# Graph attention kernel, second layer: absent pairs through TensorE, the search for a block's top in four parts, the negation on GpSimd, three loads issued during the projection

## The chip, the cores and the metric

The kernel runs on one core of one Trainium2 chip. The metric is the device time of one execution in microseconds (us), of which the median over several runs is taken.

## The reference

6250 nodes with 128 channels, 200000 edges sorted by target. Two graph attention layers, each followed by a layer norm of input plus layer. The change lies in the second layer (`_L1_gnn_ref`), with 4 heads of 32 channels:

```python
H = jnp.matmul(x, W).reshape(n, HEADS, OUT_DIM).transpose(1, 0, 2)
H_s = jnp.einsum('hnd,hd->hn', H, A_left[..., 0])
H_t = jnp.einsum('hnd,hd->hn', H, A_right[..., 0])
s = H_s[:, src] + H_t[:, tgt]
s = jnp.where(s >= 0, s, ALPHA * s)
s = jnp.exp(s - jnp.max(s))
denom = jnp.zeros((HEADS, n), dtype=s.dtype).at[:, src].add(s)
alpha = s / (denom[:, src] + EPS)
agg = jnp.zeros((HEADS, n, OUT_DIM), dtype=H.dtype).at[:, src].add(alpha[..., None] * H[:, tgt])
agg = agg + jnp.matmul(x, residual_projection).reshape(n, HEADS, OUT_DIM).transpose(1, 0, 2)
```

and an elu, the sum with the input and the norm behind it. The kernel subtracts a top per block of source nodes instead of one global maximum, and corrects the small constant in the denominator for it at the end.

## The kernel before, in words

The 6250 nodes lie in 49 blocks of 128. An early stage sorts the edges into pairs of blocks (source block b, target block n); an edge of a pair gets one of 128 lanes, and a lane without an edge is an absent pair, marked by -1 in the table `SL`. Stages follow one another with a barrier between them: loading, binning, scores of the first layer, sums of the first layer (`layer0_sums`), `norm_and_project` (L1036), which turns the normed nodes and multiplies them by the weights of the second layer, `layer1` (L1157), and `elu_and_norm`.

`layer1` works in 343 steps: for each of the 49 source blocks b, 7 steps of 7 target blocks each (`GX = 7`, `PER = 7`). Five engines run their own hand-written order and meet through semaphores:

- **SP** (L1191) loads, for step u, the lanes' node numbers of 7 source-target pairs, spread to all 128 partitions (448 KB), into a ring of three (`LOADS`). Load u waits until the one-hot of step u-3 is made.
- **VectorE** (L1265): in iteration t it makes the one-hot of step t+10 (`make`, L1209), in one iteration in seven searches the top of a block (`find_top`, L1212), weighs the gathered rows by the softmax weights (`weigh`, L1244), compares lanes (`find_lanes`, L780), in one in seven negates the block's top (`negate`, L1233), and takes the low half of three messages (`take_low`, L1252). `find_top` for block b stands in iteration 7b-2, ahead of `weigh`: it marks absent lanes by -1e30 (L1217), reduces the three parts of the scores out of two PSUM banks (L1219, twice), takes max(0.2 s, s) (L1225), adds the marks (L1227) and takes the maximum over the free axis (L1228).
- **GpSimd** (L1280): for each block the all-reduce of the top over the partitions (L1289), then for block b-1 two additions of low sums (L1283, L1284), which wait for ScalarE's copies, then the subtraction of 1 from X (L1292).
- **TensorE** (L1343): in iteration t the scores of step t+9 (`add_scores`, 14 matmuls of 12 columns, L1306 and L1307), the gather of step t+1 (21 matmuls of 128 columns, L1316), the sums of step t (`add_up`, 4 matmuls in fp32, L1330, of which the last needs ScalarE's last message, and 3 matmuls of halves, L1335). The first scores of a block wait until `find_top` of the block before has read the banks.
- **ScalarE** (L1399): in iteration t the high halves (L1379), the message of the seventh target block (`weigh_last`, 4 instructions, L1385), in one iteration in seven the exponent (L1361, it waits for the negated top), the copy of weights (L1370), the widening of the lane one-hots to fp32 (L1374); once per block the staging of the block's lanes (L1354) and the taking of the sums (L1393 to L1395).

`weigh` of a block's first step waits for the exponent. TensorE's `add_up` waits for `weigh`, and TensorE, VectorE and ScalarE are at most two steps apart through double buffers for gathered rows, messages and lane one-hots. The one-hots have a ring of 11.

A first matmul with `start=True` opens a bank's sums; later ones with `start=False` add.

## Time and profile before

| | |
|---|---|
| median of 3 runs | 3372.64 us (3370.05 to 3385.1) |
| the profiled execution | 3371.61 us, its span 3369.8 us |
| mean granted TensorE clock | 0.968 |
| busy: TensorE, weight loads, VectorE, ScalarE, GpSimd | 91%, 83%, 92%, 81%, 5% |
| `layer1` | 2274 to 3315 us |
| `norm_and_project` | 2232 to 2274 us |

The profile shows one execution. Busy time is that of instructions; PE is TensorE's matmuls, DVE VectorE, ACT ScalarE, POOL GpSimd. A granted clock of 1.00 is 2.4 GHz, 0.50 is 1.2 GHz. "Issue" is time in which an engine waited for nothing that the profile shows. Instructions on one engine overlap at their ends, so a start-to-start distance is a little shorter than a duration.

### The profile page before, as it was taken

The numbers are of one execution on the slowest core, as the hardware profiler recorded it, in microseconds if no ns is written. First come the engines' busy times: TensorE is split into PE (matmuls) and PEld (weight loads), VectorE is DVE, ScalarE is ACT, GpSimd is POOL, SyncE is SP. The second block draws the span as 40 slices with busy tenths as digits, with TensorE's granted clock in tenths as the row PEclk, the third lists the DMA queues.
The fourth block names the chain that finished last, engine by engine and source line by source line (L and its number), as shares of the span: only waits on it lengthen the run. The fifth ranks groups of instructions, "written<-read, shape, count | busy, mean of one in ns | idle before, by whom it ended". The sixth has DMA issues, their size and how long they took to land. (4 is left out here: it accounts for less than half of the span.)

```text
span 3369.8 us, 100973 instructions
## 1 busy us (share of the span) xinstructions
PE 3073.6 (91%) x39974; PEld 2791.6 (83%) x39974; DVE 3095.1 (92%) x5054; ACT 2725.8 (81%) x6802; POOL 159.1 (5%) x252
## 2 busy tenths in 40 slices
PE   4777689999999999699999999987999999999995
PEld 3666577777777777599999999977999999999994
DVE  7999879998999999899999999978999999999997
ACT  4989777777877777699999999975777777777777
POOL 0000000000000000000000000000111111111110
PEclk9999899999999999799999999998999999999998
DMA  2000022222222222244333333305444445444441
GB/s 63 12 15 12 9 96 90 84 90 85 90 84 85 90 84 72 55 96 96 97 97 97 96 97 97 96 30 182 159 156 156 158 156 158 157 156 158 156 144 40
DMA packets 173164, 333.01 MB, mean 99 GB/s; under 512 B 54849, under 2 KB 108693, under 8 KB 172690
## 3 DMA queue, kind: packets, MB, share of 16 engines
q1 hardware_dynamic: 172690, 326.50, 31.6%
q8 instruction: 321, 5.26, 0.6%
q14 instruction: 153, 1.25, 0.1%
HBM read 320.77 MB, written 5.66 MB: 97 GB/s over the span
## 5 line engine op out<-in xcount | busy, mean ns | idle before, releaser
L942 PE MATMUL l_gathered<-xp,l_src_onehot 128*128 128x128 bf16 x7203 | 466.9, 221 | 11.2 <-DVE l_src_onehot L855 11.2
L647 PE MATMUL sc_z<-sc_onehot,pq 128*128 128x256 f32 (+1 forms) x2450 | 426.5, 296 | 54.5 <-DVE sc_leaky L568 44.9
L1316 PE MATMUL l_gathered<-hp,l_onehot 128*128 128x128 bf16 x7203 | 459.0, 219 | 0.0
L736 ACT ACTIVATE sc_leaky<-sc_z 128x1024 f32<-128x1024 f32 (+3 forms) x325 | 310.1, 954 | 153.0 <-PE sc_z L651 96.3
L942 PEld LDWEIGHTS l_gathered<-xp,l_src_onehot 128*128 128x128 bf16 x7203 | 407.8, 99 | 26.2 <-DVE l_src_onehot L855 11.6
L780 DVE TENSOR_TENSOR l_lane<-iota_b,l_lane_pairs 128x896 bf16<-128x896 bf16 x686 | 421.7, 615 | 0.0
L1330 PE MATMUL l_acc<-e,l_lane_wide 128*128 128x132 f32 x2744 | 399.3, 286 | 16.5 <-ACT e L1385 16.3
L568 DVE SCALAR_TENSOR_TENSOR sc_leaky<-sc_z,sc_leaky 128x1024 f32<-128x1024 f32 (+3 forms) x325 | 369.9, 1138 | 45.6 <-ACT sc_leaky L736 42.2
L1316 PEld LDWEIGHTS l_gathered<-hp,l_onehot 128*128 128x128 bf16 x7203 | 406.7, 98 | 0.4
L651 PE MATMUL sc_z<-sc_onehot,pq 128*128 128x256 f32 (+1 forms) x2450 | 401.0, 286 | 0.0
L647 PEld LDWEIGHTS sc_z<-sc_onehot,pq 128*128 128x128 f32 x2450 | 340.7, 194 | 69.3 <-issue 68.2
L1330 PEld LDWEIGHTS l_acc<-e,l_lane_wide 128*128 128x128 f32 x2744 | 338.4, 190 | 32.9 <-ACT e L1385 25.9
L1379 ACT CAST l_message_halves<-e 128x396 fp32r<-128x396 f32 x343 | 179.2, 522 | 213.2 <-DVE e L1244 211.6
L651 PEld LDWEIGHTS sc_z<-sc_onehot,pq 128*128 128x128 f32 x2450 | 345.7, 196 | 0.0
L1244 DVE TENSOR_TENSOR e<-l_gathered,l_weight 128x768 f32<-128x768 f32 x343 | 326.8, 953 | 10.7 <-PE l_gathered L1316 3.9
L1374 ACT CAST l_lane_wide<-l_lane 128x896 fp32r<-128x896 bf16 x343 | 329.1, 959 | 0.0
L988 ACT CAST l_lane_wide<-l_lane 128x896 fp32r<-128x896 bf16 x343 | 322.2, 939 | 4.0 <-DVE l_lane L780 4.0
L559 DVE TENSOR_SCALAR sc_onehot<-placed,part 128x1536 fp32r<-128x1536 uint8 (+3 forms) x325 | 310.8, 957 | 3.8 <-DMA placed<-edge_rows 3.7
L953 PE MATMUL l_acc<-l_messages,l_lane_wide 128*128 128x128 f32 x2058 | 305.9, 285 | 5.7 <-ACT l_messages L997 5.7
L997 ACT ACTIVATE l_messages<-l_gathered,e 128x128 f32<-128x128 f32 x1029 | 301.5, 363 | 0.0
L869 DVE TENSOR_TENSOR l_message_halves<-l_messages,l_message_halves 128x512 fp32r<-128x512 f32 x343 | 237.5, 692 | 53.1 <-ACT l_message_halves L1003 48.3
L1385 ACT ACTIVATE e<-l_gathered,l_weight 128x32 f32<-128x32 f32 x1372 | 280.6, 286 | 0.0
(233 smaller groups left out, 6064.3 us busy)
## 6 DMA issues: line engine op xcount, KB each, us to landing
l_got<-edge_rows_wide SPq DMA_DIRECT2D x343, 448.0 KB, 3.7
l_got<-edge_rows_src SPq DMA_DIRECT2D x343, 224.0 KB, 3.2
placed<-edge_rows SPq DMA_DIRECT2D x144, 512.0 KB, 3.7
out_dram<-X SPq DMA_DIRECT2D x12, 256.0 KB
edge_rows<-bin_bytes SPq DMA_DIRECT2D x98, 6.1 KB
edge_rows_wide<-bin_rows SPq DMA_DIRECT2D x98, 12.2 KB
placed<-edge_rows SPq DMA_DIRECT2D x24, 64.0 KB, 2.8
placed<-edge_rows SPq DMA_DIRECT2D x6, 256.0 KB, 3.6
```

The source lines that it names most:

```text
L559: nc.vector.tensor_scalar(hot[:, r % HOTS, 0:early, :, 0:nw, :], bytes_of(r)[:, 0:early, :, 0:nw, :], k.part1[:, 0:1], None, ALU.is_equal) ...
L568: nc.vector.scalar_tensor_tensor(out=y, in0=z, scalar=ALPHA, in1=y, op0=ALU.mult, op1=ALU.add).then_inc(s["leaky"], 1)
L647: nc.tensor.matmul(z[:, b, 0:nw, :], PQ[:, b0 + b, q, 0:C], hot[:, r % HOTS, b, 0, 0:nw, :], start=(b == u and q == 0), stop=False)
L651: ins = nc.tensor.matmul(z[:, u:u + v, n, :], PQ[:, 2 * pair + n, q, C:2 * C], hot[:, r % HOTS, u:u + v, 1, n, :], start=False, stop=(n == ...
L736: nc.scalar.activation(y, z, ACT.Relu, scale=1.0 - ALPHA).then_inc(s["positive"], 1)
L780: return nc.vector.tensor_tensor(out.rearrange("p i (u v) -> p i u v", v=2), k.iota_b[:].rearrange("p (u v) -> p u v", v=2).unsqueeze(1).t ...
L942: ins = nc.tensor.matmul(gps[:, t % 2, i * P:(i + 1) * P], hot[:, t % RING, i, :], parts[:, g * GX + i, q, :], start=(q == 0), stop=(q == 2))
L988: nc.scalar.copy(lane_wide[:, t % 2], lane[:, t % 2]).then_inc(s["lane_wide"], 1)
L1244: nc.vector.tensor_tensor(msg[:, t % 2, 0:w, 0:C].rearrange("p i (e d) -> p i e d", e=HEADS), gps[:, t % 2, 0:w * P].rearrange("p (i e d) ...
L1316: ins = nc.tensor.matmul(gps[:, t % 2, i * P:(i + 1) * P], dst_hot[:, t % RING, i, :], hp[:, g * GX + i, q, 0:C], start=(q == 0), stop=(q ...
L1330: nc.tensor.matmul(acc[:, b % 2, 0:CW], lane_wide[:, t % 2, i, :].bitcast(F32), msg[:, t % 2, i, :], start=(g == 0 and i == SPLIT), stop=F ...
L1374: nc.scalar.copy(lane_wide[:, t % 2], lane[:, t % 2]).then_inc(s["lane_wide"], 1)
```

## The change

Absent lanes are no longer marked on VectorE. ScalarE makes a bf16 tile `absent` (Relu of the negated `SL`: 1 where a lane is absent, 0 elsewhere), once per block and two blocks ahead. TensorE opens each bank of scores with one matmul of that tile (28 or 21 target blocks by 4 heads) against -1e30 times the identity, and the score matmuls add to it. So the leaky step takes the mark with it.

The search is taken apart: the reduction of the first bank in iteration 7b-4, its leaky half in 7b-3, the reduction and leaky half of the second bank and the maximum in 7b-2, all behind `weigh`; the maximum is the last of its iteration. The semaphore `read` becomes two, one per bank.

The negation goes from VectorE to GpSimd, behind the all-reduce. The first three loads of `layer1` are issued by SP at the start of `norm_and_project`; their tile and semaphores are allocated outside `layer1`.

```diff
--- before.py
+++ after.py
@@ -1033,7 +1034,14 @@
 
-def norm_and_project(nc, k, X, mean_var, hp, R):
+def load_rows(sp, k, got, wide_rows, u):
+    b, g = divmod(u, NBK // GX)
+    sp.dma_start(got[:, u % LOADS_1].rearrange("p a x -> p (a x)"),
+         wide_rows[g, 2 * b:2 * b + 2].rearrange("a i l -> (a i l)").partition_broadcast(P)
+         ).then_inc(k.rows_loaded[u % LOADS_1], 16)
+
+
+def norm_and_project(nc, k, X, mean_var, hp, R, got, wide_rows):
@@ -1060,6 +1068,11 @@
 with nc.Block() as block:
+    @block.sync
+    def _(sp):
+        for u in range(LOADS_1):
+            load_rows(sp, k, got, wide_rows, u)
+
@@ -1168,13 +1181,13 @@
 s = {n: ctx.semaphore("l1_" + n) for n in (
-    "chain", "const", "hot", "scored", "read", "top", "all", "negated", "exp", "staged", "lane", "lane_wide", "gathered",
+    "chain", "const", "hot", "scored", "absent", "first_read", "last_read", "first_lifted", "last_lifted", "top", "all", "negated", "exp", "staged", "lane", "lane_wide", "gathered",
     "messages", "last_message", "weights", "high", "low", "added", "taken", "summed")}
-loaded = [ctx.semaphore(f"l1_loaded{h}") for h in range(LOADS)]
-got = sb("got", [P, LOADS, 2, GX * P], BF16)
+loaded = k.rows_loaded
...
 src_hot, dst_hot = hot[:, 0:2], hot[:, 2:]
-win, absent = sb("lane_pairs", [P, 2, NB, 2], BF16), sb("absent", [P, NB])
+win = sb("lane_pairs", [P, 2, NB, 2], BF16)
+absent, never = sb("absent", [P, 2, NB], BF16), sb("never", [P, P], BF16)
@@ -1187,13 +1200,9 @@
     def _(sp):
-        for u in range(R):
-            b, g = divmod(u, PER)
-            if u >= LOADS:
-                sp.wait_ge(s["hot"], u - LOADS + 1)
-            sp.dma_start(got[:, u % LOADS].rearrange("p a x -> p (a x)"),
-                         wide_rows[g, 2 * b:2 * b + 2].rearrange("a i l -> (a i l)").partition_broadcast(P)
-                         ).then_inc(loaded[u % LOADS], 16)
+        for u in range(LOADS, R):
+            sp.wait_ge(s["hot"], u - LOADS + 1)
+            load_rows(sp, k, got, wide_rows, u)
@@ -1209,29 +1218,39 @@
 
-        def find_top(b):
-            dve.wait_ge(s["staged"], b + 1)
-            dve.wait_ge(s["scored"], (b + 1) * PER)
+        def take_scores(b, bank, i, j):
+            nc.vector.tensor_reduce(
+                parts[:, i:j, :], sps[:, bank, 0:(j - i) * HP].rearrange("p (i q e) -> p i e q", q=3, e=HEADS),
+                AX.X, ALU.add).then_inc(s["last_read" if bank else "first_read"], 1)
+
+        def lift(b, bank, i, j):
+            dve.wait_ge(s["last_read" if bank else "first_read"], b + 1)
...
                 dve.wait_ge(s["exp"], b - 1)
-            nc.vector.tensor_scalar(absent[:], win[:, b % 2, :, 0], 0.0, NEVER, ALU.is_lt, ALU.mult)
-            for bank, i, j in ((0, 0, FIRST), (1, FIRST, NB)):
-                ins = nc.vector.tensor_reduce(
-                    parts[:, i:j, :], sps[:, bank, 0:(j - i) * HP].rearrange("p (i q e) -> p i e q", q=3, e=HEADS),
-                    AX.X, ALU.add)
-            ins.then_inc(s["read"], 1)
-            dve.wait_ge(s["read"], b + 1)
-            flat, sc = parts[:].rearrange("p i e -> p (i e)"), score[:, b % 2]
-            ch.link(nc.vector.scalar_tensor_tensor(out=sc.rearrange("p i e -> p (i e)"), in0=flat, scalar=ALPHA, in1=flat,
-                                                   op0=ALU.mult, op1=ALU.max))
-            ch.link(nc.vector.tensor_tensor(sc, sc, absent[:].unsqueeze(2).to_broadcast([P, NB, HEADS]), ALU.add))
-            nc.vector.tensor_reduce(top[:, b % 2:b % 2 + 1], sc.rearrange("p i e -> p (i e)"), AX.X, ALU.max
+            flat = parts[:, i:j, :].rearrange("p i e -> p (i e)")
+            nc.vector.scalar_tensor_tensor(out=score[:, b % 2, i:j, :].rearrange("p i e -> p (i e)"), in0=flat, scalar=ALPHA,
+                                           in1=flat, op0=ALU.mult, op1=ALU.max
+                                           ).then_inc(s["last_lifted" if bank else "first_lifted"], 1)
+
+        def take_first(b):
+            dve.wait_ge(s["scored"], b * PER + FIRST // GX)
+            if b >= 1:
+                dve.wait_ge(s["first_lifted"], b)
+            take_scores(b, 0, 0, FIRST)
+
+        def take_last(b):
+            dve.wait_ge(s["scored"], (b + 1) * PER)
+            if b >= 1:
+                dve.wait_ge(s["last_lifted"], b)
+            take_scores(b, 1, FIRST, NB)
+
+        def find_top(b):
+            dve.wait_ge(s["first_lifted"], b + 1)
+            dve.wait_ge(s["last_lifted"], b + 1)
+            if b >= 2:
+                dve.wait_ge(s["all"], b - 1)
+            nc.vector.tensor_reduce(top[:, b % 2:b % 2 + 1], score[:, b % 2].rearrange("p i e -> p (i e)"), AX.X, ALU.max
                                     ).then_inc(s["top"], 1)
-
-        def negate(b):
-            dve.wait_ge(s["all"], b + 1)
-            nc.vector.tensor_scalar(neg[:, b % 2:b % 2 + 1], k.m_all[:, b:b + 1], -1.0, None, ALU.mult
-                                    ).then_inc(s["negated"], 1)
@@ -1259,22 +1278,29 @@
 
+        nc.vector.tensor_scalar(never[:], k.ident_b[:], NEVER, None, ALU.mult).then_inc(s["const"], 1)
...
                 make(t + AHEAD + 1)
+            if t >= 0:
+                weigh(t)
+            if (t + 4) % PER == 0 and 0 <= (t + 4) // PER < NB:
+                take_first((t + 4) // PER)
+            if (t + 2) % PER == 0 and 0 <= (t + 2) // PER < NB:
+                take_last((t + 2) // PER)
+            if 0 <= t + 1 < R:
+                find_lanes(t + 1)
+            if (t + 3) % PER == 0 and 0 <= (t + 3) // PER < NB:
+                lift((t + 3) // PER, 0, 0, FIRST)
+            if (t + 2) % PER == 0 and 0 <= (t + 2) // PER < NB:
+                lift((t + 2) // PER, 1, FIRST, NB)
+            if t >= 0:
+                take_low(t)
...
                 find_top((t + 2) // PER)
-            if t >= 0:
-                weigh(t)
-            if 0 <= t + 1 < R:
-                find_lanes(t + 1)
-            if (t + 1) % PER == 0 and 0 <= (t + 1) // PER < NB:
-                negate((t + 1) // PER)
-            if t >= 0:
-                take_low(t)
@@ -1283,10 +1309,15 @@
 
-        pool.wait_ge(s["const"], 1)
+        pool.wait_ge(s["const"], 2)
...
             nc.gpsimd.partition_all_reduce(k.m_all[:, b:b + 1], top[:, b % 2:b % 2 + 1], P, RMAX).then_inc(s["all"], 1)
+            pool.wait_ge(s["all"], b + 1)
+            if b >= 2:
+                pool.wait_ge(s["exp"], b - 1)
+            nc.gpsimd.tensor_scalar(neg[:, b % 2:b % 2 + 1], k.m_all[:, b:b + 1], -1.0, None, ALU.mult
+                                    ).then_inc(s["negated"], 1)
@@ -1294,17 +1325,31 @@
     def _(pe):
+        def exclude(b, bank, i, j):
+            nc.tensor.matmul(sps[:, bank, 0:(j - i) * HP].rearrange("p (i c) -> p i c", c=HP)[:, :, 0:HEADS], never[:],
+                             absent[:, b % 2, i:j].unsqueeze(2).to_broadcast([P, j - i, HEADS]), start=True, stop=False,
+                             skip_group_check=True)
+
...
             b, g = divmod(u, PER)
+            if g == 0:
+                pe.wait_ge(s["absent"], b + 1)
+                if b >= 1:
+                    pe.wait_ge(s["first_read"], b)
+                exclude(b, 0, 0, FIRST)
+            if g == FIRST // GX:
+                if b >= 1:
+                    pe.wait_ge(s["last_read"], b)
+                exclude(b, 1, FIRST, NB)
             pe.wait_ge(s["hot"], u + 1)
-            if g == 0 and b >= 1:
-                pe.wait_ge(s["read"], b)
...
                 o = sps[:, bank, at * HP:(at + 1) * HP]
-                nc.tensor.matmul(o, dst_hot[:, u % RING, i, :], hp[:, n, :, C + HEADS:C + 2 * HEADS], start=True, stop=False)
-                ins = nc.tensor.matmul(o, src_hot[:, u % 2, i, :], hp[:, b, :, C:C + HEADS], start=False, stop=True)
+                nc.tensor.matmul(o, dst_hot[:, u % RING, i, :], hp[:, n, :, C + HEADS:C + 2 * HEADS], start=False, stop=False,
+                                 skip_group_check=True)
+                ins = nc.tensor.matmul(o, src_hot[:, u % 2, i, :], hp[:, b, :, C:C + HEADS], start=False,
+                                       stop=(n in (FIRST - 1, NB - 1)), skip_group_check=True)
@@ -1337,6 +1382,7 @@
 
+        pe.wait_ge(s["const"], 1)
@@ -1350,8 +1396,12 @@
                 act.wait_ge(s["lane"], (b - 1) * PER)
-                act.wait_ge(s["top"], b - 1)
             nc.scalar.copy(win[:, b % 2], k.SL[:, 0, 0:NB, b].unsqueeze(2).to_broadcast([P, NB, 2])).then_inc(s["staged"], 1)
+
+        def find_absent(b):
+            if b >= 2:
+                act.wait_ge(s["scored"], (b - 1) * PER)
+            nc.scalar.activation(absent[:, b % 2], k.SL[:, 0, 0:NB, b], ACT.Relu, scale=-1.0).then_inc(s["absent"], 1)
@@ -1394,6 +1444,8 @@
 
+        find_absent(0)
+        find_absent(1)
@@ -1406,6 +1458,8 @@
                 widen(t + 1)
+            if t >= 0 and (t - 2) % PER == 0 and (t - 2) // PER + 2 < NB:
+                find_absent((t - 2) // PER + 2)
```

## Rows read from the trace of the kernel before

**Rows 1.** Busy time by stretch: start:end, length, busy (instructions) per engine, PEclk, DMA share, GB/s
```profile
2400.00:2600.00 200.00, 196.99 (x3109) 190.45 (x3106) 194.37 (x336) 158.89 (x526) 25.36 (x39) 1.00 0.49 158
```

**Rows 2.** Waits, 2330 to 3270 us: engine line <- releaser: us, times, longest
```profile
PE l_acc L1330 <- ACT e L1385: 15.1, 45, 0.3
```

**Rows 3.** PE timeline, one block: start us, us, engine line (idle before)
```profile
2788.77 1.33 PE L1316 MATMUL l_gathered<-hp,l_onehot 128*128 128x128 bf16 x21
...
2791.64 1.33 PE L1316 MATMUL l_gathered<-hp,l_onehot 128*128 128x128 bf16 x21
...
2795.28 1.33 PE L1316 MATMUL l_gathered<-hp,l_onehot 128*128 128x128 bf16 x21
```

**Rows 4.** DVE timeline, the search of one block and an ordinary step
```profile
2789.92 0.19 DVE L1217 TENSOR_SCALAR l_absent<-l_lane_pairs 128x49 f32<-128x49 bf16 x1
2790.01 0.83 DVE L1219 TENSOR_REDUCE l_score_parts<-l_scores 128x112 f32<-128x336 f32 x2
2790.87 0.36 DVE L1225 SCALAR_TENSOR_TENSOR l_score<-l_score_parts 128x196 f32<-128x196 f32 x1
...
2791.66 0.36 DVE L1228 TENSOR_REDUCE l_top<-l_score 128x1 f32<-128x196 f32 x1
2791.94 0.95 DVE L1244 TENSOR_TENSOR e<-l_gathered,l_weight 128x768 f32<-128x768 f32 x1
...
2797.22 0.96 DVE L1244 TENSOR_TENSOR e<-l_gathered,l_weight 128x768 f32<-128x768 f32 x1
...
2798.77 0.57 DVE L1252 TENSOR_TENSOR l_message_halves<-e,l_message_halves 128x396 fp32r<-128x396 f32 x1
...
2799.85 0.95 DVE L1244 TENSOR_TENSOR e<-l_gathered,l_weight 128x768 f32<-128x768 f32 x1
```

**Rows 5.** ACT timeline, the exponent and the last messages of a step
```profile
2796.66 0.47 ACT L1361 ACTIVATE l_weight<-l_score,l_negated 128x196 f32<-128x196 f32 x1
...
2798.64 0.82 ACT L1385 ACTIVATE e<-l_gathered,l_weight 128x32 f32<-128x32 f32 x4
```

**Rows 6.** POOL timeline, blocks 0 and 1
```profile
2295.91 0.60 POOL L1289 PARTITION_ALL_REDUCE block_top<-l_top  x1 [65.56 <-DVE l_top L1228]
2305.07 0.92 POOL L1292 TENSOR_SCALAR X<-X 128x128 f32<-128x128 f32 x1 [8.55 <-issue]
2313.62 0.38 POOL L1289 PARTITION_ALL_REDUCE block_top<-l_top  x1 [7.63 <-DVE l_top L1228]
2324.97 0.76 POOL L1283 TENSOR_TENSOR S<-S,l_low_sums 128x128 f32<-128x128 f32 x1 [10.97 <-ACT den L1395]
```

**Rows 7.** Source lines of GpSimd: xcount, duration ns min/median/max, first and last start
```profile
L1283 POOLq MODIFY_POOL_CONFIG  x96: 82/83/83, 2314.0 to 3291.6; - x96
...
L1284 POOL TENSOR_TENSOR den<-den,l_low_sums x49: 203/522/527, 2325.7 to 3314.6; 128x4 f32<-128x4 f32 x49
...
L1289 POOLq MODIFY_POOL_CONFIG  x98: 5/7/11, 2274.8 to 3284.8; - x98
...
L1292 POOLq MODIFY_POOL_CONFIG  x2: 83/83/83, 2296.5 to 2296.5; - x2
```

**Rows 8.** DVE timeline, start of the layer: first and ninth one-hot, first weighing
```profile
2278.84 0.69 DVE L1209 TENSOR_SCALAR l_onehot<-l_got,part 128x1792 bf16<-128x1792 bf16 x1 [3.76 <-DMA l_got<-edge_rows_wide]
...
2292.98 0.69 DVE L1209 TENSOR_SCALAR l_onehot<-l_got,part 128x1792 bf16<-128x1792 bf16 x1 [1.41 <-DMA l_got<-edge_rows_wide]
...
2297.83 0.96 DVE L1244 TENSOR_TENSOR e<-l_gathered,l_weight 128x768 f32<-128x768 f32 x1 [0.36 <-PE l_gathered L1316]
```

**Rows 9.** PE around the gap before the projection: start:end, length, busy, PEclk, DMA share, GB/s
```profile
2222.00:2229.00 7.00, 6.70 (x76) 1.00 0.01 2
...
2235.00:2238.20 3.20, 3.00 (x13) 0.50 0.00 0
```

**Rows 10.** PE timeline, the same gap
```profile
2235.20 1.67 PE L1105 MATMUL np_turned_ps<-ident,X 128*128 128x128 f32 x6 [5.84 <-DVE X L1069]
```

**Rows 11.** ACT timeline, last stage
```profile
3339.03 1.28 ACT L2254 ACT_TABLE_LOAD   x1
```

More of the change, by code:

```diff
@@ L100 @@
 GX = 7
+LOADS_1 = 3
 R_BYTES = 4 * P
@@ L1154, in _, with layer1 @@
                     take_middle(g)
-def layer1(nc, k, hp, wide_rows, spare, X, S, den4):
+def layer1(nc, k, hp, got, wide_rows, spare, X, S, den4):
     NB, PER, AHEAD = NBK, NBK // GX, 9
     R = NB * PER
-    RING, LOADS = AHEAD + 2, 3
+    RING, LOADS = AHEAD + 2, LOADS_1
     CW, HP, FIRST = C + HEADS, 3 * HEADS, 28
@@ L2307, in gnn_program @@
         k.x_loaded = ctx.semaphore("x_loaded")
+        k.rows_loaded = [ctx.semaphore(f"rows_loaded{h}") for h in range(LOADS_1)]
         k.w1_all = sb("w1_all", [P, 2 * C + 2 * HEADS])
@@ L2344, in binned_layer1 @@
                 hp = scope.enter_context(nc.sbuf_tensor("hp", [P, k.NI, 3, C + 2 * HEADS], BF16))
-                norm_and_project(nc, k, X, mean_var, hp, R)
-                layer1(nc, k, hp, wide_rows, e0[:].rearrange("p a b -> p (a b)"), X, S, den4)
+                got = scope.enter_context(nc.sbuf_tensor("rows_got", [P, LOADS_1, 2, GX * P], BF16))
+                norm_and_project(nc, k, X, mean_var, hp, R, got, wide_rows)
+                layer1(nc, k, hp, got, wide_rows, e0[:].rearrange("p a b -> p (a b)"), X, S, den4)
         either(nc, "layer0", binned, 1, binned_layer0,
```

## The prediction

> **What bounds the kernel now.** I read the busy time by stage first, then the waits, then the timelines of one block. The change touches the second layer (2274 us to the end) and the first microseconds of the projection before it. In a stretch of 200 us inside that layer TensorE is busy 197.0 us and VectorE 194.4 us at a granted clock of 1.00, while GpSimd has 25 us of work [rows 1]. So TensorE and VectorE are both nearly full, and who waits for whom decides. The only repeated wait of TensorE is for ScalarE's last message, once per block [rows 2].
>
> The PE timeline gives the size. From one gather to the next takes 2.87 us (2788.77 to 2791.64); in the step with the search it takes 3.64 us (2791.64 to 2795.28) [rows 3]. A block is 7 steps: 6 x 2.86 + 3.64 = 20.80 us, of which 0.78 us is loss, 48 times.
>
> The DVE timeline says why [rows 4]. An ordinary VectorE step takes 2.63 us (2797.22 to 2799.85), less than TensorE's. But the search is one unbroken run ahead of the weighing: 2789.92 to 2791.94, 2.02 us. From the start of a weighing ScalarE needs 2.24 us until its last message is made (2797.22 to 2798.64 + 0.82) [rows 4, 5]. The search makes the weighing about 1.8 us late, TensorE loses 0.78 us, so some 1.0 us of lateness is free.
>
> **The search, part by part.** Removed from VectorE per block: the comparison L1217 (0.19), the addition L1227 (as long as the leaky step beside it), the negation, and the waits between dependent instructions. Kept: two reductions (0.83 together), the leaky step (0.36, now in two halves, between 0.18 and 0.36 each; I take 0.25 for the first and 0.2 for the second), the search for the top (0.36) [rows 4]. They now lie in three steps, and none stands before the weighing of its own step. The most added between two weighings is 0.36 + 0.2 + 0.36 = 0.9 us, in the third of these steps, after VectorE has gained 0.23 us on TensorE in each step without them. That stays under the free 1.0 us. Taken alone this removes all of the 0.78 us: 48 x 0.78 = 37 us.
>
> **Absent pairs on TensorE.** Two matmuls per block, with 112 and 84 columns. The gather does 21 matmuls of 128 columns in 1.33 us, its end included, 0.06 each [rows 3]; by columns the two cost 0.09 us. The floor is zero (hidden in a stall), the ceiling 0.78 us, the whole gain of the search part: two matmuls would then cost more than half a gather, which nothing suggests. I take 0.09, the nearest shape: 49 x 0.09 = 4.4 us if TensorE bounds. Their buffers are released two steps earlier (reads of scores) and three (the rectified row), so their waits cost nothing unless VectorE is more than two steps behind; then the scores and gathers queued behind them on TensorE would wait too.
>
> **The Relu on ScalarE**, 49 columns, is smaller than the exponent (196 columns, 0.47 us [rows 5]), once a block. ScalarE is idle for 41 of 200 us [rows 1], some 0.6 us per step, and the Relu stands in a step that has neither staging, exponent nor taking. I take nothing; if that cover went, it would be at most 0.47 x 49 = 23 us. Relu and Exp alternate in the last stage with no table load until L2254 asks for Sqrt [rows 11], so no table is reloaded. If it were, two loads of 1.28 us per block would come.
>
> **Loads issued early.** Today the first one-hot is made at 2278.84 and the ninth at 2292.98, each after its load [rows 8]. With three loads there already, the first is made at about 2275.1, and the fourth load is issued some 3.6 us sooner; the spacing after that is the loads' own. The ninth one-hot then comes at about 2289.4. SP issues nothing else during the projection and nothing in it waits for a DMA; the three transfers (448 KB each) have some 40 us to land, so they cost nothing. They also pass no other queue; if they were late, the first one-hot would wait as before. The first top is found at about 2290.9 in place of 2295.69 (the end of the ninth one-hot, 2293.67, and the 2.02 us of the search).
>
> **The negation on GpSimd.** This is the term that decides. Before, a block's top goes VectorE, GpSimd (all-reduce), VectorE (negation), ScalarE (exponent). The negation moves onto GpSimd, right behind the all-reduce. In the trace GpSimd runs two instructions MODIFY_POOL_CONFIG ahead of each all-reduce (98 at L1289) and two more right after it, booked on the next ordinary instruction (96 at L1283, 2 at L1292) [rows 7]. So it changes its code twice per block. What does the change back cost? Once the trace shows it: in block 0 nothing is waited for, the all-reduce ends at 2296.51, and L1292 starts at 2305.07 after 8.55 us of "issue" [rows 6]. From block 1 on, the next ordinary instruction waits 10.97 us for ScalarE anyway [rows 6], which hides 8.55 us. The new negation has no such cover: behind it stand ScalarE's exponent, then VectorE's weighing L1244 of the block's first step, then TensorE's sum.
>
> Is 8.55 us paid once or in each block? For each block: the four instructions recur in all 49, and ordinary code had been in use before (the first layer's additions on GpSimd, L928), so its return was not a first load. For once: only one exposed case. I take 8.55 each time.
>
> The Trainium skill, GPSIMD Engine Reference, section Instruction dispatch, says that the first call to a freshly loaded kernel additionally pays about 6 us (5.95 measured) with no visible instruction. The mechanism agrees with the trace, the size does not; by 5.95 the sum below, without its clock term, would be about 3506 us, an estimate.
>
> **The chain.** Let a block's first weighing start at 0. VectorE reaches the weighing of its sixth step (the one with the end of the search) after 5 x 2.63 = 13.15 us plus 0.3 (of the 0.7 us of first reduction and first leaky half, 0.4 us lies in the gap that the subtraction L1252, starting 1.55 us after its weighing, leaves while it waits for ScalarE) [rows 4]: 13.45. From there to the end of the top: 1.55 + 0.4 + 0.49 + 0.36 = 2.8, so 16.25. Then: 0.14 for the hand-over to GpSimd, 0.38 for the all-reduce [rows 6], 8.56 for the code, 0.3 for the negation (bounds 0.20 and 0.52, a 4-column addition on GpSimd [rows 7]), 0.47 for the exponent [rows 5], some 0.1 for hand-overs: 9.95. The next block's first weighing starts at 26.2 us, where TensorE alone would need 7 x 2.86 + 0.09 = 20.12.
>
> **The clock.** TensorE then idles some 5.8 us in each block. A gap of the same length stands in the trace: after 5.84 us without a matmul it resumed at 2235.20, and the granted clock was 0.50 (1.2 GHz) until 2238.2, 3.0 us more; before the gap it had been busy at 2.4 GHz [rows 9, 10]. Half of 3.0 us is 1.5 us of lost work; 0.6 us of it falls into the wait for the last message, 0.2 us into VectorE's own lateness; 0.7 us stays. Bounds: 0 (clock up again at once) and 2.2 us (low for twice as long). Period: 26.95 us.
>
> **The sum.** Start of the layer: top at 2290.9, + 0.2 + 0.60 + 8.56 + 0.3 + 0.47 + 0.1 gives the first weighing at 2301.15, where it was at 2297.83 [rows 8]: +3.3 us (the 4.7 us won by the loads go into the code change). Then 48 x (26.95 - 20.80) = +295 us. 3371.6 + 298 = 3670 us. The profiled execution stands 1 us below the median of the three runs, so no correction is due. With no clock loss it is 3371.6 + 3.3 + 48 x 5.4 = 3634; with the upper clock bound 3742. If the change of code took 7.3 us in later blocks (the all-reduce's own comes ready in at most the 7.63 us that GpSimd idles before it in block 1 [rows 6]), it is about 3610.
>
> **Rivals.**
> - *The code returns for free after the first time* (8%). For it: only one exposed case; against it: the recurring instructions [rows 7]. Then the start still costs 3.3 us, and each block runs at 20.12 us: 48 x 0.68 = 33 us gained, 3371.6 + 3.3 - 32.6 = 3342 us. Faster. The point that decides: the chain is 26.2 - 8.56 = 17.65 us and the code's time; it passes TensorE's 20.12 us from 2.5 us on, and each further microsecond costs 48.
> - *The return costs something between* (4%), 4 to 7 us, because later loads run faster than the one seen: 3410 to 3590 us; slower.
> - *The negation is cheap, but a new wait or the two matmuls eat the gain* (2%): TensorE waits for the rectified row or for the split reads; 0.7 us per block puts it at 3365 to 3380, no change.
>
> **How the numbers follow.** The forecast has 86%. Its own range covers 7.3 to 8.9 us of code change and 0 to 2.2 us of clock loss: 3560 to 3760, which holds it 19 times in 20, so 8 times in 10 in all. A measurement of this kernel tells 0.5% (17 us) from no change. Faster: 8% for the free return, and 2% for a cover that I overlooked. Same: 2%. Slower: 88%.
>
> **What would show it.** After the change: on GpSimd the negation preceded by some 8.5 us of "issue" in all 49 blocks; ScalarE's exponent waiting for GpSimd, 6 us each; VectorE's L1244 waiting for the exponent; TensorE idle 5 to 6 us per block with the granted clock at 0.50 in patches, a mean below 0.9 in a layer that shows 1.00 now; no more wait of 0.33 us in the search step; the first one-hot at 2275. The forecast is wrong if the "issue" appears only once: then the time is below the one of before. It is wrong in size if the clock stays at 1.00 or falls for longer.

## The result, and the profile after

| | before | after |
|---|---|---|
| median of 6 runs each, us | 3373.30 (3368.47 to 3390.03) | 3684.76 (3681.21 to 3687.29) |
| ratio, 95% interval | | 1.0924 [1.0904, 1.0944] |
| profiled run, us (span) | 3371.61 (3369.8) | 3681.21 (3679.4) |

The changed kernel is 311 us slower; 3670 had been forecast, between 3560 and 3760.

Busy time by stretch, kernel after (start:end, length, busy (instructions) of PE, PEld, DVE, ACT, POOL, then PEclk, DMA share, GB/s), the same stretch as [rows 1]:

```profile
2400.00:2600.00 200.00, 161.77 (x2312) 157.79 (x2313) 141.14 (x239) 122.60 (x405) 14.91 (x36) 0.86 0.35 117
```

Every engine has lost work in the same time, and the granted clock is 0.86 where it was 1.00. No engine is full, so the layer is now bound by a chain of waits. They are, from 2400 to 3400 us (us in total, times, longest):

```profile
POOL l_negated L1319 <- issue: 287.1, 37, 8.5
...
DVE e L1263 <- issue: 230.1, 37, 7.0
ACT l_weight L1411 <- POOL l_negated L1319: 227.6, 37, 6.9
...
PE l_acc L1375 <- ACT l_lane_wide L1424: 178.4, 37, 5.6
```

These are four views of one event. 37 blocks lie in that stretch, and each line stands 37 times. GpSimd stands idle before the negation without a wait that the trace shows, 287.1 / 37 = 7.76 us each; ScalarE's exponent waits 6.2 us for that negation; VectorE's first weighing waits 6.2 us (shown as "issue"; in block 0, below, the profile names the exponent); TensorE's sum waits 4.8 us. [Rows 2] had 45 waits of 0.33 us in its place.

The GpSimd timeline, kernel after, blocks 0 to 2 (start us, us, engine line operation, in brackets the idle time before it):

```profile
2285.93 0.38 POOL L1315 PARTITION_ALL_REDUCE block_top<-l_top  x1 [59.28 <-DVE l_top L1252]
2293.49 0.26 POOL L1319 TENSOR_SCALAR l_negated<-block_top 128x1 f32<-128x1 f32 x1 [7.17 <-issue]
...
2311.89 0.69 POOL L1315 PARTITION_ALL_REDUCE block_top<-l_top  x1 [17.61 <-DVE l_top L1252]
2320.66 0.26 POOL L1319 TENSOR_SCALAR l_negated<-block_top 128x1 f32<-128x1 f32 x1 [8.08 <-issue]
...
2339.11 0.70 POOL L1315 PARTITION_ALL_REDUCE block_top<-l_top  x1 [10.19 <-DVE l_top L1252]
2347.41 0.26 POOL L1319 TENSOR_SCALAR l_negated<-block_top 128x1 f32<-128x1 f32 x1 [7.60 <-issue]
```

This answers [rows 6]. There the idle time before the next ordinary instruction was called "issue" only in block 0; now it is in every block. The two instructions MODIFY_POOL_CONFIG that [rows 7] shows at L1283 have moved to the negation's line, 98 of them, two for each of the 49 blocks (source lines of GpSimd: count, duration ns min/median/max, first and last start):

```profile
L1319 POOLq MODIFY_POOL_CONFIG  x98: 82/83/83, 2286.3 to 3595.1; - x98
L1319 POOL TENSOR_SCALAR l_negated<-block_top x49: 260/260/261, 2293.5 to 3602.2; 128x1 f32<-128x1 f32 x49
```

One block boundary on VectorE, kernel after: the end of the search, the first weighing of the next block, the top after that, and the weighing behind it:

```profile
2611.39 0.35 DVE L1252 TENSOR_REDUCE l_top<-l_score 128x1 f32<-128x196 f32 x1
...
2621.76 0.96 DVE L1263 TENSOR_TENSOR e<-l_gathered,l_weight 128x768 f32<-128x768 f32 x1 [6.80 <-issue]
...
2639.01 0.35 DVE L1252 TENSOR_REDUCE l_top<-l_score 128x1 f32<-128x196 f32 x1
...
2648.58 0.96 DVE L1263 TENSOR_TENSOR e<-l_gathered,l_weight 128x768 f32<-128x768 f32 x1 [6.00 <-issue]
```

The chain closes here. From the end of one top (2611.74) to the weighing it releases is 10.0 us, from that weighing to the end of the next top (2639.36) 17.6 us, then 9.2 us again. On the mean of blocks 2 to 46 the two stretches are 9.45 and 17.85 us. The mean distance between the starts of the all-reduces of blocks 2 to 46, which I call the period, is 27.30 us, and was 20.81 us. 48 x 6.49 = 311 us, the whole difference.

### The profile page after: what moved, and what is told of

Read it like the earlier page. It is cut to its first block and busy times, and to the rows that moved or that the text cites. A ratio compares the mean times of both kernels' runs of the same rounds, so it can differ in the third digit from the quotient of the medians.

```text
span 3679.4 us, 101361 instructions
## 1 busy us (share of the span) xinstructions
PE 3169.8 (86%) x40072; PEld 2894.6 (79%) x40072; DVE 3055.4 (83%) x4957; ACT 2737.1 (74%) x6851; POOL 135.8 (4%) x301
## 5 line engine op out<-in xcount | busy, mean ns | idle before, releaser
L1375 PE MATMUL l_acc<-e,l_lane_wide 128*128 128x132 f32 x2744 | 433.1, 306 | 237.9 <-ACT l_lane_wide L1424 237.6
L1375 PEld LDWEIGHTS l_acc<-e,l_lane_wide 128*128 128x128 f32 x2744 | 378.2, 211 | 245.2 <-DVE e L1263 244.7
L1361 PE MATMUL l_gathered<-hp,l_onehot 128*128 128x128 bf16 x7203 | 502.2, 230 | 0.0
L1361 PEld LDWEIGHTS l_gathered<-hp,l_onehot 128*128 128x128 bf16 x7203 | 448.9, 104 | 0.5
```

The source lines that it names most:

```text
L1361: ins = nc.tensor.matmul(gps[:, t % 2, i * P:(i + 1) * P], dst_hot[:, t % RING, i, :], hp[:, g * GX + i, q, 0:C], start=(q == 0), stop=(q ...
L1375: nc.tensor.matmul(acc[:, b % 2, 0:CW], lane_wide[:, t % 2, i, :].bitcast(F32), msg[:, t % 2, i, :], start=(g == 0 and i == SPLIT), stop=F ...
```

## The experiments

Theory A: the change of GpSimd's code back to ordinary instructions, behind each all-reduce, costs 7 to 8.5 us and stands on the path once it has no cover; the half clock that follows adds to it. Rival B: something else in the change (the matmuls for absent pairs, the split search, the early loads) costs the time. Rival C: the cost is that of any second instruction on GpSimd, or of one more hand-over to it, and not of the change of code.

All ratios are to the kernel before, run beside them on the same chip (medians 3373.3, 3368.7, 3369.6 and 3369.1 us). The period is reckoned from the trace of one execution, as above. Medians of different groups can differ by a few us, as those of the kernel before do, so small differences between runs are read from the period and not from the medians alone.

| run | us, median | ratio [95%] | period, us |
|---|---|---|---|
| after | 3684.76 | 1.0924 [1.0904, 1.0944] | 27.30 |
| neg_dve | 3331.40 | 0.9889 [0.9870, 0.9907] | 20.11 |
| before_neg_pool | 3572.24 | 1.0582 [1.0552, 1.0612] | 24.91 |
| two_reduces | 3331.65 | 0.9888 [0.9871, 0.9904] | 20.10 |
| warm | 3612.69 | 1.0723 [1.0705, 1.0741] | 25.74 |
| late_loads | 3337.61 | 0.9897 [0.9877, 0.9917] | 20.11 |
| one_search | 3343.33 | 0.9926 [0.9901, 0.9951] | 20.37 |
| split_only | 3332.95 | 0.9886 [0.9865, 0.9906] | 20.07 |
| lead | 3477.23 | 1.0305 [1.0274, 1.0337] | 23.11 |
| neg_act | 3329.83 | 0.9884 [0.9868, 0.9901] | 20.11 |
| act_marks | 3324.71 | 0.9874 [0.9857, 0.9890] | 20.01 |

**neg_dve: the changed kernel with the negation back on VectorE.**

```
-  pool.wait_ge(s["all"], b + 1)              # GpSimd, behind the all-reduce
-  pool.wait_ge(s["exp"], b - 1)
-  nc.gpsimd.tensor_scalar(neg..., k.m_all..., -1.0, None, ALU.mult).then_inc(s["negated"], 1)
+  def negate(b):                             # VectorE, in the step before the block
+      dve.wait_ge(s["all"], b + 1)
+      nc.vector.tensor_scalar(neg..., k.m_all..., -1.0, None, ALU.mult).then_inc(s["negated"], 1)
```

> The changed kernel with only the negation put back on VectorE, between the lane comparison and the low halves of the step before the exponent. Theory (the change back to ordinary code on GpSimd, some 7.8 us, is on the path once per block): all of the loss goes and the rest of the change shows its gain: start of the layer about 5 us shorter, block period 20.12 us in place of 20.80, so 3335 us, 3325 to 3345; no idle gap of TensorE over 1 us in the layer, clock 1.00. Rival (matmuls of absent pairs, split reads or Relu cost something too): the time stays above 3345. Rival (GpSimd's part is only a share of the loss, the split search breaks something else): above 3400.

Measured: 3331.40 us. One instruction per block of 128 x 1 elements on another engine is worth 353 us, and without it the change is a gain of 37 us. Busy time by stretch, neg_dve:

```profile
2400.00:3200.00 800.00, 800.00 (x12898) 785.49 (x12895) 784.51 (x1354) 658.06 (x2188) 113.62 (x157) 1.00 0.51 162
```

TensorE is busy 800.00 of 800 us at full clock; in the kernel before it was 787.07 over the same stretch. So the rest of the change does what it says and TensorE is the bound. The code still changes in this kernel, as its GpSimd timeline shows:

```profile
2286.95 0.60 POOL L1322 PARTITION_ALL_REDUCE block_top<-l_top  x1 [59.87 <-DVE l_top L1252]
2296.52 0.56 POOL L1325 TENSOR_SCALAR X<-X 128x128 f32<-128x128 f32 x1 [8.97 <-issue]
```

The same idle time stands there, but nobody waits behind it. Rival B falls.

**before_neg_pool: the kernel before, with this one part of the change.**

```
-  def negate(b): ...                         # VectorE
+  pool.wait_ge(s["all"], b + 1)              # GpSimd, behind the all-reduce
+  pool.wait_ge(s["exp"], b - 1)
+  nc.gpsimd.tensor_scalar(neg..., k.m_all..., -1.0, None, ALU.mult).then_inc(s["negated"], 1)
```

> The kernel before with only the negation moved to GpSimd behind the all-reduce. Theory: the loss comes from this part alone. The search now ends 2.02 us after VectorE's fifth step, so the top is known at 5 x 2.63 + 2.02 = 15.2 us (plus 1 to 1.4 us for the slow clock), the chain adds 9.6 us: period 25.8 to 26.3 us against 20.80, 48 x 5.2 = 250 us, and 8 us at the start: 3620 to 3650 us. Rival (the loss needs the later place of the search for the top, behind the low halves): under 3500 us.

Measured: 3572.24 us, the right direction, less than expected. Its waits, 2400 to 3400 us:

```profile
POOL l_negated L1286 <- issue: 288.1, 40, 7.9
...
ACT l_weight L1359 <- POOL l_negated L1286: 129.9, 40, 3.9
...
PE l_acc L1328 <- ACT l_lane_wide L1372: 94.7, 40, 3.0
```

The change of code costs 288.1 / 40 = 7.20 us here, against 7.76 in the kernel after, and the all-reduce ahead of it 0.38 us against 0.70. On the mean of blocks 2 to 46, from the end of a top to the weighing is 8.58 us, where 9.6 had been expected, and from there to the end of the next top 16.32 us, within the 16.2 to 16.6 expected. So the miss lies in the chain through GpSimd, which was put 1.0 us too high. TensorE waits 2.4 us, where it waited 4.8 in the kernel after, and the mean clock from 2400 to 3200 us is 0.94, where it was 0.87. The stretch from the weighing to the next top is 1.5 us shorter than in the kernel after; how much of this is the clock and how much the place of the search, no run separates.

**two_reduces: a second all-reduce in place of the negation.** The top is already the same in all partitions, so reducing it again leaves it unchanged; ScalarE makes the negation.

```
-  nc.gpsimd.tensor_scalar(neg..., k.m_all..., -1.0, None, ALU.mult).then_inc(s["negated"], 1)
+  nc.gpsimd.partition_all_reduce(again..., k.m_all..., P, RMAX).then_inc(s["again"], 1)
+  nc.scalar.activation(neg..., again..., ACT.Copy, scale=-1.0)   # ScalarE, ahead of the exponent
```

> The changed kernel, the negation on GpSimd replaced by a second all-reduce of the result (the same kind of code, no ordinary instruction), and the sign turned by ScalarE ahead of the exponent. Theory (the price is the change of code, not a second dependent GpSimd instruction): two all-reduces follow each other within 1.5 us, the chain is ready before ScalarE wants it: 3337 us, 3325 to 3350. Rival (any instruction of GpSimd behind the all-reduce, or the wait on its own semaphore, costs the 7.8 us): 3650 to 3700 us.

Measured: 3331.65 us, the same as neg_dve. The GpSimd timeline:

```profile
2609.20 0.69 POOL L1315 PARTITION_ALL_REDUCE block_top<-l_top  x1 [8.23 <-DVE l_top L1252]
2609.99 0.35 POOL L1319 PARTITION_ALL_REDUCE l_again<-block_top  x1
2618.76 0.87 POOL L1309 TENSOR_TENSOR S<-S,l_low_sums 128x128 f32<-128x128 f32 x1 [8.41 <-ACT den L1446]
```

A second instruction in the same place, with the same wait for the first and a hand-over more behind it, begins 0.10 us after the first one's end, in all 49 blocks. No MODIFY_POOL_CONFIG is booked on its line; the pair (83 ns each, 96 in all) stands at the ordinary addition L1309 behind it, and block 0's first ordinary instruction has 8.67 us of "issue" ahead of it. What costs is the step from the all-reduce to an ordinary instruction. Rival C falls. What GpSimd does in that time no view shows; "change of code" goes by the name of the instruction that stands there.

**warm: TensorE kept busy through the gap.** In the second step of each block the 21 matmuls of the gather are done five times, each repeat writing the same sums; 84 matmuls more per block.

```
-  for i in range(GX):
+  for again in range(5 if g == 1 else 1):
+      for i in range(GX):
```

> The changed kernel; TensorE repeats the gather of each block's second step four more times (84 matmuls, some 4.7 us) in the gap in which it waits for the block's first weighing; results are the same. Theory (of the 6.4 us per block some 1.3 us is the slow clock after the gap): the granted clock stays at 1.00 in the layer and the period falls from 27.2 to about 26.0 us: 3610 to 3640 us. Rival (the clock costs nothing, since VectorE sets the pace after the gap anyway): 3680 us. Rival (the added matmuls do not fit the gap): slower than 3685 us.

Measured: 3612.69 us, 72 us less than after, though TensorE does more. The PE timeline, warm:

```profile
2604.40 6.02 PE L1362 MATMUL l_gathered<-hp,l_onehot 128*128 128x128 bf16 x105
2611.61 1.53 PE L1376 MATMUL l_acc<-e,l_lane_wide 128*128 128x132 f32 x8 [1.19 <-ACT l_lane_wide L1425]
```

The gap shrinks from 4.8 us on the mean in the kernel after to 1.2 us at most, in 21 of the 31 blocks from 2400 to 3200 us, and the granted clock from 2400 to 3200 us is 1.00. The period falls from 27.30 to 25.74 us. All of it lies between the first weighing and the next top: 17.85 us there becomes 16.26, while the stretch from the top to the weighing stays (9.45 and 9.48). So 1.56 us of each block (75 us) was the half clock, and the other 4.9 us above 20.81 is the chain itself.

**late_loads: neg_dve with the first three loads back in the layer.**

```
-  for u in range(LOADS_1):                   # SyncE, projection stage
-      load_rows(sp, k, got, wide_rows, u)
...
-  for u in range(LOADS, R):
-      sp.wait_ge(s["hot"], u - LOADS + 1)
+  for u in range(R):
+      if u >= LOADS: sp.wait_ge(s["hot"], u - LOADS + 1)
```

> The changed kernel with the negation on VectorE (run neg_dve), and the first three loads issued by the second layer itself again. Theory: the early loads shorten the start of the layer by 4 to 6 us and nothing else: 3335 to 3339 us, where neg_dve gave 3331.4. Rival (the transfers overlap with nothing that matters): 3331.

Measured: 3337.61 us, 6.2 us above neg_dve, at the same period. The first weighing is at 2297.51, against 2290.43 in neg_dve. The intervals of the two ratios overlap, so the trace has to decide. As the layer starts 1.5 us apart in the two executions, the distance from the layer's first MEMSET is the cleaner measure: 23.6 us against 18.1, so 5.6 us. The early loads are a gain paid once.

**one_search: neg_dve with the search in one piece ahead of the weighing**, as in the kernel before, with absent pairs still on TensorE.

```
+  if (t + 2) % PER == 0 ...: take_first; take_last; lift 0; lift 1; find_top
   if t >= 0: weigh(t)
-  ... take_first at t + 4, take_last at t + 2, lifts at t + 3 and t + 2, find_top behind take_low
```

> neg_dve with the whole search for the top in one place again, ahead of the weighing of its step; absent pairs still through TensorE, so the search has no comparison and no addition. Theory: the run on VectorE is some 1.55 us in place of 2.02, of which 0.2 us of wait and 1.0 us of slack are free: TensorE loses about 0.3 us per block in place of 0.78, 3346 us, 3340 to 3352. Rival (the two matmuls alone bring the gain, since the search is short enough): 3332. Rival (taking the search apart brings all of it): 3365.

Measured: 3343.33 us, 11.9 us above neg_dve; period 20.37, and 0.26 x 48 = 12.5 us. TensorE's 0.78 us of loss has shrunk to about 0.26 by the removal of the comparison and the addition alone, 0.55 us of search (0.19 + 0.36 by [rows 4]).

**split_only: neg_dve with absent pairs back on VectorE.**

```
-  exclude(b, 0, 0, FIRST); exclude(b, 1, FIRST, NB)        # TensorE
-  nc.scalar.activation(absent..., ACT.Relu, scale=-1.0)    # ScalarE
+  mark(b)                                                  # VectorE, comparison behind the first lift
+  nc.vector.tensor_tensor(sc, sc, absent..., ALU.add)      # VectorE, ahead of the top
```

> neg_dve with absent pairs marked on VectorE again (comparison in the step of the first leaky half, addition behind the last), the search still over three steps, no matmul for absent pairs. Theory: VectorE has 0.55 us more per block, in total 7 x 2.63 + 1.7 = 20.1 us against TensorE's 20.04, and 1.3 us of it at one place: between no loss and 0.3 us per block, 3327 to 3345 us. Rival (the matmuls for absent pairs are needed for the gain): 3355 or more.

Measured: 3332.95 us, no difference from neg_dve (3331.40) that can be told. Either part alone takes most of the 0.78 us away, and the split takes all of it; the matmuls for absent pairs then bring nothing more, and cost next to nothing (20.11 against 20.07 us per block).

**lead: the changed kernel, with the search three steps earlier** (AHEAD 9 to 12), so that some 8 us more lie between the top and the weighing. The Relu for absent pairs on ScalarE moves with it, which the cut below leaves out.

```
-  NB, PER, AHEAD = NBK, NBK // GX, 9
+  NB, PER, AHEAD = NBK, NBK // GX, 12
-  take_first at t + 4, first lift at t + 3, take_last, last lift and find_top at t + 2
+  take_first at t + 7, first lift at t + 6, take_last, last lift and find_top at t + 5
```

> The changed kernel (negation on GpSimd), with scores made 12 steps ahead in place of 9 and the whole search three iterations earlier, so that the top is known some 8.6 us before it is now. Theory in its simple form (only the latency from top to exponent counts): the 10 us chain fits into the lead and the time falls to 3335 to 3345 us. My own refinement: GpSimd must also change its code back for the all-reduce, behind the last of its work for the block before; from the first weighing at 0 that work ends near 8 us, the other code needs up to 7 us, then 0.4 + 7.8 + 0.8: a period of about 24 us, 3520 to 3560 us, GpSimd waiting for its own code both ways. Rival (a VectorE or GpSimd cost other than latency): unchanged near 3685.

Measured: 3477.23 us, 208 us better than after, and still 3% slower than before. The simple form, that an earlier top hides the cost, is wrong; the refinement is right in kind and too high in size. The GpSimd timeline, lead:

```profile
2630.34 0.38 POOL L1315 PARTITION_ALL_REDUCE block_top<-l_top  x1 [6.40 <-issue]
2638.17 0.26 POOL L1319 TENSOR_SCALAR l_negated<-block_top 128x1 f32<-128x1 f32 x1 [7.45 <-issue]
2645.56 0.46 POOL L1309 TENSOR_TENSOR S<-S,l_low_sums 128x128 f32<-128x128 f32 x1 [7.12 <-ACT den L1445]
...
2646.14 0.56 POOL L1323 TENSOR_SCALAR X<-X 128x128 f32<-128x128 f32 x1
2652.64 0.38 POOL L1315 PARTITION_ALL_REDUCE block_top<-l_top  x1 [5.94 <-issue]
```

GpSimd no longer waits for the top. It now pays for the change in the other direction too, 5.9 us, and between the two it waits 7.12 us for ScalarE's sums of the block before, which ScalarE takes two steps behind the exponent that GpSimd has just released. 0.38 + 7.45 + 0.26 + 7.12 + 1.1 + 5.94 = 22.3 us (the mean period is 23.11): GpSimd is a ring of its own, longer than TensorE's 20.1 us, with 2 us of work in it.

**neg_act: the negation on ScalarE, right ahead of the exponent.**

```
-  nc.gpsimd.tensor_scalar(neg..., k.m_all..., -1.0, None, ALU.mult).then_inc(s["negated"], 1)
+  nc.scalar.activation(neg..., k.m_all..., ACT.Copy, scale=-1.0).then_inc(s["negated"], 1)   # ScalarE
```

> The changed kernel with the negation on ScalarE, right ahead of the exponent. Theory: ScalarE has some 0.6 us free per step and the top is known long before, so the place of the negation does not matter as long as it is not on GpSimd behind a change of code: 3331 us, as neg_dve, within 3326 to 3336. Rival (ScalarE's extra instruction and its wait on itself, 0.3 to 0.4 us ahead of the exponent, make the first weighing late): 3340 or more.

Measured: 3329.83 us, as neg_dve within what can be told. VectorE is relieved of the negation at no cost.

**act_marks: the best version found.** split_only, with the mark for absent pairs made by ScalarE and subtracted by VectorE.

```
-  nc.vector.tensor_scalar(absent..., win..., 0.0, NEVER, ALU.is_lt, ALU.mult)
+  nc.scalar.activation(absent..., k.SL..., ACT.Relu, scale=NEVER)    # ScalarE
-  ch.link(nc.vector.tensor_tensor(sc, sc, absent..., ALU.add))
+  ch.link(nc.vector.tensor_tensor(sc, sc, absent..., ALU.subtract))
```

> split_only with the mark made by ScalarE (Relu of -1e30 times the table: 1e30 where absent) and subtracted on VectorE; no matmul for absent pairs, negation on VectorE, early loads. Theory: the layer is bound by TensorE, and the two matmuls cost 0.09 us per block, so this takes 4 us off neg_dve: 3327 us, 3323 to 3332. Rival (VectorE's added subtraction makes it late): 3332 or more.

Measured: 3324.71 us (3323.95 to 3329.50), 1.3% faster than before. Busy time by stretch, act_marks:

```profile
2400.00:3200.00 800.00, 800.00 (x12878) 785.59 (x12877) 789.12 (x1401) 661.78 (x2200) 115.44 (x160) 1.00 0.50 163
```

TensorE is full, and without the two extra matmuls a block costs it 20.01 us. The step from neg_dve, 0.10 x 48 = 5 us, is near the 4.4 us that the prediction had put on those matmuls, though split_only, which has no such matmuls either, does not show it (20.07). VectorE's comparison has moved in act_marks too; which of the two counts, no run separates.

## Why the prediction was right, point by point

- **The code change is paid in each block.** Right, and it was the step that decided. 49 of 49 blocks show it. The price was taken from one case, 8.55 us; the measured mean of the 49 is 7.74 (7.03 to 8.57). The all-reduce ahead of it took 0.70 us in later blocks, not 0.38, and the negation 0.26, not 0.3. Together, from the start of the all-reduce to the start of the negation, 8.43 us on the mean against 8.94. The Trainium skill, GPSIMD Engine Reference, section Instruction dispatch, has 5.95 us for the first call of a freshly loaded kernel, with no visible instruction. The trace agrees with it in kind and not in size or number: a pause without a visible instruction, 7.7 us on the mean, at every return. The estimate worked out from the page's figure, 3506 us without a clock term, was 179 us too low.
- **From the first weighing to the next top.** Forecast 16.25 us and 0.7 us for the clock; measured 17.85 on the mean. The 16.25 was right: in warm, at full clock, the stretch is 16.26 us. Here lies the larger of the two terms that were mis-sized, *the clock*. The granted clock around the gap, kernel after, TensorE alone (start:end, length, busy, PEclk, DMA share, GB/s):

```profile
2617.50:2620.90 3.40, 0.11 (x3) 0.95 0.02 7
2620.90:2623.00 2.10, 0.00 (x0) 0.50 0.00 0
2623.00:2627.40 4.40, 4.38 (x39) 0.50 0.35 102
2627.40:2631.00 3.60, 3.60 (x60) 1.00 0.34 135
```

TensorE resumed at 2623.01 after 5.40 us and ran at 1.2 GHz until about 2627.4: 4.4 us. Over blocks 1 to 48 this is 4.9 us on the mean (4.1 to 6.1), where [rows 9, 10] had shown 3.1 us after a gap of about the same length. What the prediction did not look at is when the clock fell. In the kernel before, in that gap:

```profile
2229.40:2231.40 2.00, 0.00 (x0) 1.00 0.00 0
2231.40:2235.20 3.80, 0.00 (x1) 0.50 0.05 13
2235.20:2238.30 3.10, 3.10 (x13) 0.51 0.00 0
```

There the clock had been at half for 3.8 us when TensorE resumed, and here for 1.9 us on the mean (2.5 in the block shown), so more of the half clock fell on work. TensorE's timeline of this block has the price in it:

```profile
2616.28 1.33 PE L1361 MATMUL l_gathered<-hp,l_onehot 128*128 128x128 bf16 x21
2623.01 2.10 PE L1375 MATMUL l_acc<-e,l_lane_wide 128*128 128x132 f32 x8 [5.40 <-ACT l_lane_wide L1424]
...
2626.01 1.97 PE L1361 MATMUL l_gathered<-hp,l_onehot 128*128 128x128 bf16 x21
```

  The gather of 1.33 us takes 1.97, and VectorE's third weighing of the block waits 0.92 us for it. The warm run prices the whole at 1.56 us per block, against 0.7 taken and 2.2 as the upper bound. 0.9 us too little here and 0.5 us too much in the code change and all-reduce left a period of 27.30 us against 26.95. That the two errors have opposite signs is luck: with the clock alone put right the forecast would have been some 3710 us. By the prediction's own terms its upper clock bound is 3634 + 48 x 2.2 = 3740 us, and not 3742, which changes nothing.
- **The start.** Forecast +3.3 us, measured +0.1: from the layer's first instruction to the first weighing 23.2 us (2271.18 to 2294.34), before 23.1 (2274.76 to 2297.83 [rows 8]). The top came 1.6 us sooner than forecast, because the ninth one-hot follows the first by 12.4 us and not by the 14.3 of the forecast, and block 0's change of code and all-reduce were 1.6 us cheaper. VectorE at that point:

```profile
2271.52 2.02 DVE L1218 TENSOR_SCALAR l_onehot<-rows_got,part 128x1792 bf16<-128x1792 bf16 x3
...
2283.95 0.69 DVE L1218 TENSOR_SCALAR l_onehot<-rows_got,part 128x1792 bf16<-128x1792 bf16 x1 [0.28 <-DMA rows_got<-edge_rows_wide]
...
2294.34 0.96 DVE L1263 TENSOR_TENSOR e<-l_gathered,l_weight 128x768 f32<-128x768 f32 x1 [5.23 <-ACT l_weight L1411]
```

  The first three one-hots follow at once, as forecast: their loads had landed.
- **The search alone gives 37 us.** The total was right, its parts were not quite these. neg_dve gains 37.3 us, of which the steady blocks give 48 x 0.70 = 34 us (0.78 less what the matmuls take) and the early loads 6 us; the two add up to a little more than the total. "0.9 us" for the most added between two weighings was 1.0 (0.41 + 0.24 + 0.35 in the third step), just what was free.
- **Matmuls and Relu.** Forecast 0.09 us per block and nothing. One block's step with a matmul for absent pairs ahead of its scores is 2.91 us long (gathers at 2607.65 and 2610.56), the ordinary one before it 2.86 (2604.79), so 0.05 each and 0.1 for the two. The Relu takes 0.32 us, and no wait names it. Relu and Exp alternate in all blocks, and neg_dve has one ACT_TABLE_LOAD (1.28 us) between 2270 and 3250 us: no table is reloaded.
- **The signs named.** "Issue" in all 49 blocks, the exponent waiting 6 us, TensorE idle 4.5 to 5.6 us (4.8 on the mean, 5.40 in the block shown) in patches of half clock, and a mean clock of 0.87 in the layer: all there. Only VectorE's weighing shows its wait as "issue", and not under the exponent's name, in nearly all blocks.
- **The sum.** 48 x (27.30 - 20.81) = 311.5 us and 0.1 at the start, against 295 + 3.3. The rivals are gone: a free return would have given 3342, and 4 to 7 us of code change at most 3590.

## What to carry to other kernels

An engine with little work is not therefore free: look at what an instruction placed on it stands behind, and who waits for it. In these runs an ordinary operation on GpSimd right behind an all-reduce paid 6.7 to 9.0 us every time that no wait covered it, so keep the two kinds apart on a dependent path, or give such a small operation to an engine that already stands in the chain (neg_act cost nothing). "Issue" in front of an instruction that waits for nothing is the sign; if it hides in another wait, as in [rows 6], it becomes visible only once something that others wait for is put right behind the all-reduce.

## What the runs showed of the hardware that was not expected

- The change of code costs in both directions: 6.7 to 9.0 us from all-reduce to ordinary, and 5.7 to 6.8 us back (6.0 on the mean of 47 blocks), seen only in lead, where no wait covers it.
- It varies between kernels, for no reason that these runs show: 7.20 us in before_neg_pool, 7.76 in after. The all-reduce took 0.38 us in one and 0.70 in the other. This stays open; no run was made on it.
- After gaps of 4.5 to 5.6 us in the layer the granted clock stayed at half for 4.9 us of work on the mean, and for 3.1 us after one of 5.84 us before the projection. It had fallen 1.9 us and 3.8 us before the work resumed. 84 matmuls more in each block made the kernel 72 us faster.
